# Routed expert tiles: the up product with the weights stationary and 128 tokens moving

## What is computed

```python
shared = silu(xf @ shared_w1.T) * (xf @ shared_w2.T) @ shared_w3.T
scores = sigmoid(xf @ router_w.T)
_, top_idx = top_k(scores + expert_bias, 2)          # 8 experts
...
# each token passes through its two experts, weighted by its gate:
# gate * ((silu(x @ w1_e.T) * (x @ w2_e.T)) @ w3_e.T),  256 hidden units per expert
```

## Time and profile before

| | |
|---|---|
| median of 3 executions | 1747.06 us (1745.62 to 1749.57) |
| the profiled execution | 1750.36 us, span 1748.3 us |
| mean granted TensorE clock | 0.984 |
| busy, share of the span: PE, DVE, ACT, POOL | 94%, 65%, 49%, 39% |
| tile steps, first pass | about 257 to 436 us |
| tile steps, second pass | about 1030 to 1217 us |

### The profile page before, as it was taken

The page is one execution under the profiler, slowest core; times in us unless marked ns, Lnnn a source line. Parts: engine busy times, 40 slices in busy tenths (PEclk is TensorE's granted clock), DMA queues, the critical chain, the costliest instruction groups (busy, mean ns, idle before and its releaser), DMA issues.

```text
span 1748.3 us, 42002 instructions
## 1 busy us (share of the span) xinstructions
PE 1650.5 (94%) x14972; PEld 1109.8 (63%) x14973; DVE 1142.2 (65%) x2498; ACT 857.5 (49%) x1475; POOL 682.4 (39%) x655
## 2 busy tenths in 40 slices
PE   6999999999989999989899999999799979998999
PEld 3565656666567767665555656666466657776666
DVE  6677766666466666657765556665577477777675
ACT  4355434443466566644344334443366455664764
POOL 2342323443122222132333324433244587887243
PEclk9999999999989999999999999999899999998999
DMA  7132323332211111003210123332332033131011
GB/s 251 49 108 83 106 74 103 109 111 91 52 38 36 24 24 24 1 1 94 85 38 34 39 67 111 110 112 83 80 67 42 1 75 74 40 76 39 14 36 48
DMA packets 90149, 115.82 MB, mean 66 GB/s; under 512 B 9296, under 2 KB 76400, under 8 KB 90032
## 3 DMA queue, kind: packets, MB, share of 16 engines
q1 hardware_dynamic: 68624, 70.25, 14.5%
q0 software_dynamic: 21408, 43.93, 9.0%
HBM read 66.24 MB, written 47.90 MB: 65 GB/s over the span
## 4 chain that ended last, share of the span: by engine, by line
PE 57%; DVE 6%; POOL 4%; ACT 3%; issue 2%; DMA 0%; DVEq 0%; SPq 0%; ACTq 0%; POOLq 0%
PE ps L1675 10%; PE ps L1677 10%; PE ps L1676 10%; PE ps L1909 3%; PE ps L1908 3%; PE ps L1691 2%; PE ps L2006 2%; PE ps L1890 2%; PE ps L1891 2%; PE ps L2163 2%; PE ps L2145 1%; PE ps L2011 1%; PE ps L2133 1%; POOL work L746 1%; PE ps L1970 1%
## 5 line engine op out<-in xcount | busy, mean ns | idle before, releaser
L703 POOL DMA_INDIRECT routed<-work x142 | 136.1, 959 | 234.9 <-DVE work L1431 229.8
L1675 PE MATMUL ps<-later_hi,work 128*128 (+1 forms) x632 | 203.2, 322 | 1.2 <-ACT work L1044 1.0
L1676 PE MATMUL ps<-later_lo,work 128*128 (+1 forms) x632 | 203.1, 321 | 0.0
L1677 PE MATMUL ps<-later_hi,work 128*128 (+1 forms) x632 | 203.0, 321 | 0.0
L1675 PE MATMUL ps<-xt_hi,wsh 128*128 128x512 f16 x512 | 194.9, 381 | 4.7 <-DVEq L1185 2.2
L1676 PE MATMUL ps<-xt_lo,wsh 128*128 128x512 f16 x512 | 194.9, 381 | 0.0
L1677 PE MATMUL ps<-xt_hi,wsh 128*128 128x512 f16 x512 | 194.8, 380 | 0.0
L640 POOL TENSOR_TENSOR rstd<-mv,eps 128x4 f32<-128x4 f32 x49 | 15.2, 309 | 409.1 <-DVE mv L1140 398.4
L854 ACT ACTIVATE work<-ps 128x512 f32<-128x512 f32 x128 | 76.4, 597 | 181.5 <-PE ps L1677 170.8
L1675 PE MATMUL ps<-wsh,work 128*128 128x256 f16 x512 | 140.7, 275 | 4.8 <-ACT work L843 2.7
L1324 DVE SCALAR_TENSOR_TENSOR work<-ps,work 128x512 f32<-128x512 f32 x128 | 88.1, 689 | 84.4 <-ACT work L854 69.1
(11 more groups left out here) (246 smaller groups left out, 4257.0 us busy)
## 6 DMA issues: line engine op xcount, KB each, us to landing
work<-expert_x SPq DMA_DIRECT2D x142, 129.0 KB
yg<-in_w_later SPq DMA_DIRECT2D x9, 496.0 KB
w1q<-in_w_later SPq DMA_DIRECT2D x9, 496.0 KB
yg<-routed SPq DMA_DIRECT2D x8, 512.0 KB, 3.7
yg<-routed POOLq DMA_DIRECT2D x8, 512.0 KB, 6.0
yg<-in_w SPq DMA_DIRECT2D x8, 512.0 KB
later_hi<-routed SPq DMA_DIRECT2D x8, 512.0 KB, 3.8
later_hi<-routed POOLq DMA_DIRECT2D x8, 512.0 KB, 5.9
```

Of the source, the lines that this page charges most:

```text
L703: nc.gpsimd.indirect_dma_start(routed[:, :], bass.IndirectOffsetOnAxis(m.homes[:, i:i + 1], 0), m.t_y[:, i % 4, :], None).then_inc(s[f"til ...
L1675: nc.tensor.matmul(out_, a[0], b[0], start=start, stop=False)
L1676: nc.tensor.matmul(out_, a[0], b[1], start=False, stop=False)
L1677: return nc.tensor.matmul(out_, a[1], b[0], start=False, stop=stop)
```

## The change

The up product is made the other way round. For each of the 4 slices f of 128 units and each k, the expert's weights (128 features x 128 units) are stationary and the tile's 128 tokens move: 4 x 2 x 3 = 24 matmuls of 128 columns. The result has units on partitions, which is what the down product needs as its stationary operand, so the two second transposes, their semaphore `th_turned` and the use of PSUM banks 4 and 5 go. ACT and DVE split the product in SBUF. The gate belongs to a token, and the tokens now lie along the row in the product, so it is no longer a per-partition factor there: one small DVE operation per tile scales it into `m.gates`, and it multiplies the output at L1431, where tokens are on partitions again. The constant HS / WS takes its place in the product. DVE waits before the product for `th_lo` of two tiles earlier; ACT waits for `tile_prod` instead of `th_turned`. The arithmetic is otherwise the same.

```diff
--- before.py
+++ after.py
@@ -230,7 +230,7 @@
...
-                        "tile_hi tile_lo tile_up tile_silu tile_prod th_turned th_hi th_lo tile_down tile_y tile_out0 "
+                        "tile_hi tile_lo tile_up tile_silu tile_prod th_hi th_lo tile_down tile_y tile_out0 "
...
@@ -321,6 +321,7 @@
             m.more = r([NE, NSEQ * TPS])
             m.tile_x, m.zeros = r([4, RW]), r([RW])
             m.homes = r([TILES], I32)
+            m.gates = r([4])
             m.xn = (xn, m.tile_x)
             m.over, m.sums = r([TILES, NE]), r([2, TILES])
             m.before = r([NE, NE])
@@ -896,10 +897,10 @@
                         nc.scalar.activation(m.t_silu[:, v], ps[:, 2 + v, 0:HE], ACT.Silu, scale=1 / WS).then_inc(s["tile_silu"], 1)
                     if has(2):
                         j, v = i - 2, u % 2
-                        act.wait_ge(s["th_turned"], j + 1 + T0)
+                        act.wait_ge(s["tile_prod"], j + 1 + T0)
                         if not isinstance(j, int) or j >= 2:
                             act.wait_ge(s["tile_down"], j - 1 + T0)
-                        nc.scalar.activation(m.th_hi[:, v], ps[:, 4 + v, 0:EU * P].rearrange("p (k t) -> p k t", k=EU),
+                        nc.scalar.activation(m.th_hi[:, v].rearrange("p k t -> p (k t)"), m.t_prod[:, v],
                                              ACT.Copy).then_inc(s["th_hi"], 1)
                 each_tile(act, step, 2)
                 body(NSEQ - 1, 1)
@@ -1414,21 +1415,23 @@
                         j, v = i - 1, (u - 1) % 2
                         dve.wait_ge(s["tile_silu"], j + 1 + T0)
                         if not isinstance(j, int) or j >= 2:
-                            dve.wait_ge(s["th_turned"], j - 1 + T0)
-                        nc.vector.scalar_tensor_tensor(out=m.t_prod[:, v], in0=ps[:, 2 + v, HE:2 * HE],
-                                                       scalar=m.tile_x[:, (u - 1) % 4, D:D + 1], in1=m.t_silu[:, v],
+                            dve.wait_ge(s["th_lo"], j - 1 + T0)
+                        nc.vector.tensor_scalar(m.gates[:, (u - 1) % 4:(u - 1) % 4 + 1], m.tile_x[:, (u - 1) % 4, D:D + 1],
+                                                0.5 / (HS * HS), None, ALU.mult)
+                        nc.vector.scalar_tensor_tensor(out=m.t_prod[:, v], in0=ps[:, 2 + v, HE:2 * HE], scalar=HS / WS,
+                                                       in1=m.t_silu[:, v],
                                                        op0=ALU.mult, op1=ALU.mult).then_inc(s["tile_prod"], 1)
                     if has(2):
                         j, v = i - 2, u % 2
                         dve.wait_ge(s["th_hi"], j + 1 + T0)
-                        nc.vector.tensor_tensor(m.th_lo[:, v], ps[:, 4 + v, 0:EU * P].rearrange("p (k t) -> p k t", k=EU),
-                                                m.th_hi[:, v], ALU.subtract).then_inc(s["th_lo"], 1)
+                        nc.vector.tensor_tensor(m.th_lo[:, v].rearrange("p k t -> p (k t)"), m.t_prod[:, v],
+                                                m.th_hi[:, v].rearrange("p k t -> p (k t)"), ALU.subtract).then_inc(s["th_lo"], 1)
                     if has(3):
                         j, v = i - 3, (u - 3) % 4
                         dve.wait_ge(s["tile_down"], j + 1 + T0)
                         if not isinstance(j, int) or j >= 4:
                             dve.wait_ge(s[f"tile_out{v}"], 16 * (b - (1 if u < 3 else 0)) + in_slot(v) * earlier(n))
-                        nc.vector.tensor_scalar(m.t_y[:, v], ps[:, 6 + v % 2, 0:D], 0.5 / (WS * HS), None,
+                        nc.vector.tensor_scalar(m.t_y[:, v], ps[:, 6 + v % 2, 0:D], m.gates[:, v:v + 1], None,
                                                 ALU.mult).then_inc(s["tile_y"], 1)
                 sequences_before_tiles(dve, body)
                 assert done[0] == TAB_STEPS
@@ -1835,18 +1838,13 @@
                         pe.wait_ge(s["tile_lo"], j + 1 + T0)
                         if not isinstance(j, int) or j >= 2:
                             pe.wait_ge(s["tile_prod"], j - 1 + T0)
-                        for k in range(KT):
-                            ins = mm3(ps[:, 2 + v, :], (m.t_hi[:, v, k], m.t_lo[:, v, k]),
-                                      both(wup, ds(at + k * NE * 2 * HE, 2 * HE)), k == 0, k == KT - 1)
+                        for f in range(2 * EU):
+                            for k in range(KT):
+                                ins = mm3(ps[:, 2 + v, f * P:(f + 1) * P], both(wup, ds(at + k * NE * 2 * HE + f * P, P)),
+                                          (m.t_hi[:, v, k], m.t_lo[:, v, k]), k == 0, k == KT - 1)
                         ins.then_inc(s["tile_up"], 1)
                     if has(0):
                         pe.load(own_columns[u], m.table[0:1, ds(TILES + i, 1)])
-                    if has(2):
-                        j, v = i - 2, u % 2
-                        pe.wait_ge(s["tile_prod"], j + 1 + T0)
-                        for k in range(EU):
-                            ins = nc.tensor.transpose(ps[:, 4 + v, k * P:(k + 1) * P], m.t_prod[:, v, k * P:(k + 1) * P], ident)
-                        ins.then_inc(s["th_turned"], 1)
                     if has(3):
                         j, v = i - 3, (u - 3) % 2
                         at = columns(u, 3)
```

## The result

The changed kernel takes 1906.97 us in the median of 4 runs (1904.66 to 1910.24), beside 1747.84 for the kernel before in 4 runs on the same chip: ratio 1.0913, interval 1.0891 to 1.0934. The forecast was 1907.0. The profiled execution took 1904.66, its span is 1902.7; before it was 1750.36 and 1748.3, so the two profiled executions differ by 154.3 us, where the medians differ by 159.1.

The account below looks back on a forecast made before the run. PE's array was taken to pace each tile at 2.39 us, and after the change PE's sequencer at 3.61. Loops 146 us plus unrolled steps 18 less 4 gave +160, so 1907 us, range 1800 to 1965.

Parts of the forecast that it names:

- The bound changes from array to sequencer: Routed tiles: PE's sequencer at 3.61 us per tile exceeds the array's 2.22 and becomes the bound; chance 0.76.
- A group costs 0.235: PE's sequencer: each weight-address group takes 0.235 us; six more groups per tile add 1.41 us.
- lower bound: PE's sequencer: an address group takes at least its two instructions' own 46 + 32 = 78 ns.
- The cycle, 3.61: PE's sequencer per tile in the loops: 2.23 + 1.41 - 0.03 = 3.61 us, against 2.39 before.
- The table load: PE's sequencer between up and down groups: the load takes 0.44 us, within a stretch of 0.97.
- 146 + 18 - 4 = 160: Both tile passes: 146 us in loops, 18 in unrolled steps, less 4 for the sequencer's lead at pass starts.
- The signs: Marks of a right forecast: period near 3.6 us, ten FUSED_REGOPS per tile, "issue" idle before groups, clock 1.00.
- VectorE at nothing: DVE's added gate operation, 0.165 us per tile, costs nothing while the sequencer leads; otherwise nothing to 0.05 us per tile.
- Instruction fetch: Whole program: 83 blocks of 16 KB grow by some 5, costing nothing, at most 2 us.
- A: Rival, tile passes: the array stays the bound, groups under 0.096 us; -24 us, 1723; chance 0.09.
- B: Rival, up product: short matmuls do not hide weight loads, 81 ns per pair; +62 us, 1809; chance 0.06.
- C: Rival, tile passes: the sequencer starves PE and the clock falls to 1.2 GHz; +290 us, 2035; chance 0.07.

Follow-up runs that it names:

- run 1: Changed kernel with constant up weight addresses, every tile using expert 0's up weights: 1758.07 us, ratio 1.0018 to the kernel before.
- run 2: Kernel before with each 512-column up matmul cut into four of 128, each with its own address: 1921.25 us, ratio 1.0954.
- run 6: Low part of tile k-2 earlier: on run 1 1727.2 us, on the kernel before 1745.01, on the change with packed additions 1730.18 (1736.71 without the early order).
- Runs 3 and 4: Changed kernel with addresses packed in stretches (up 1802.4 us, up and down 1785.55), and with each address one unpacked addition (1896.43 us).
- run 7: Kernel before with only the gate moved to the output and the gates' small operation added: 1743.97 us, ratio 0.9995.
- packed_early: Whole change with addresses as packed single additions, and the low part of tile k-2 ahead of tile k-1's product: 1730.18 us, ratio 0.9919.
- fixed_early: Changed kernel with constant up addresses (expert 0) and the low part of tile k-2 ahead of tile k-1's product: 1727.2 us, ratio 0.990.
- run 5: Changed kernel with packed addresses and one six-entry table load per four tiles: 1825.04 us; with the low part earlier too, 1801.89 us.
- hoist_all: Changed kernel with the up and the down address calculations each packed in one stretch: 1785.55 us, ratio 1.019.
- packed: Whole change with addresses as packed single additions, low part in the change's own order: 1736.71 us, ratio 0.9953.
- adds: Changed kernel with the table in bytes, each address one addition and none packed: 1896.43 us, ratio 1.0864.
- hoist_load: Changed kernel with packed addresses and one table load of six entries per four tiles: 1825.04 us, ratio 1.0457.

## Why the prediction was right, point by point

**The bound changes from array to sequencer: shown.** Taking the up addresses away gives back 149 of 159 us (run 1), adding them to the kernel before costs 169 (run 2, against the 1751.82 of the kernel before on that chip), and four packed instructions for twenty turn the loss into a gain (run 6).

**A group costs 0.235: as forecast.** The groups stand 0.235 apart and there are ten per tile. I had not said what in it costs. Runs 3 and 4 show that it is the number of instructions, not of calculations, so the lower bound by the instructions' own 46 + 32 ns was no real case: a group of two lone additions of 32 ns still takes 0.226.

**The cycle, 3.61: it was 3.57** in the loop of the first pass (mean over 56 tiles) and 3.60 in the second, and 3.31 where I took 3.3 in the unrolled steps. Two terms were off, in opposite directions. The table load was too large: I took 0.44 for it from one tile; over all tiles it is 0.306, and in the array-bound kernel before it lasted 297 to 551 ns (median 308). The groups were too small: by the starts of the sequencer's instructions the ten take 2.44 us per tile in the mean, not 2.35. The sum of the passes was forecast as 146 + 18 - 4 = 160 and is 156.

**1907.0 against 1906.97: the last digits are luck.** The mechanism and the period were forecast, to about 1%. The profiled executions differ by 154.3 us and the medians by 159.1, the runs of the changed kernel alone spread over 5.6 us, and the two errors in the cycle partly cancel.

**The signs.** The period, the ten FUSED_REGOPS per tile, the groups 0.235 apart, the gap of 0.6 us between up and down and the clock of 1.00 came as written. One sign was badly chosen: idle time with "issue" before each group does not stand in the view, since the modelled ends cover it.

**VectorE at nothing: right, with a wrong reason in it.** I wrote "a few ns either way" for the output's scaling. By shape, VectorE of the changed kernel and then of the kernel before (count, busy us, mean ns, idle before):

```profile
L1434 DVE TENSOR_SCALAR work<-ps,work 128x256 f32<-128x256 f32 x142 | 68.7, 484 | 40.8 <-PE ps L1680 39.7
L1421 DVE SCALAR_TENSOR_TENSOR work<-ps,work 128x256 f32<-128x256 f32 x142 | 58.8, 414 | 0.0
L1419 DVE TENSOR_SCALAR work<-work 128x1 f32<-128x1 f32 x142 | 21.8, 154 | 174.0 <-ACT work L897 174.0
```

```profile
L1418 DVE SCALAR_TENSOR_TENSOR work<-ps,work 128x256 f32<-128x256 f32 x142 | 68.7, 484 | 98.3 <-ACT work L896 88.6 <-PE ps L1848 9.7
L1431 DVE TENSOR_SCALAR work<-ps 128x256 f32<-128x256 f32 x142 | 58.8, 414 | 5.6 <-PE ps L1677 5.5
```

The operation that takes its scalar from memory costs 484 ns and the one with a constant 414, whichever they are. The change moves that scalar from the product to the output, so 70 ns go on one side and come on the other, and only the gates' 154 ns remain. They cost nothing in the kernel before (run 7).

**Instruction fetch: right.** 83 blocks became 88, the five that I had estimated.

**The rivals.** A (array stays bound) would have shown a period near 2.2 without gaps; there are gaps, and packed_early shows what it would have taken. B (loads not hidden) is refuted by 56 ns between matmuls at 403.02 to 403.19, and not only in such a short lead: fixed_early keeps tiles of 2.21 us with PE busy in 40.00 of 40 us. The 81 ns per pair that B adds up from 25.4 and 56 would make a tile of 2.83 us. C (the clock falls) did not come in the changed kernel: the granted clock of the stretch is 1.00 with PE busy 33 of 40 us and pauses of 0.8 us at most. It did come in run 5, where PE stood for 1.8 of 2.2 us and the clock then was 0.50, so this rival was not far off. No view gives the 2.4 and 1.2 GHz that I wrote beside the clock: what the traces show is 512 columns per 0.216 us at a clock of 1.00, 2.37 per ns, and 128 columns per 0.107 us at 0.50 (run 5), 1.20 per ns.

**What stays open.** In run 1, what holds the 54th silu and PE's sequencer in both passes is not known. In hoist_all, on the same chip, the 54th silu of both passes is 1.4 us late too; in fixed_early and packed, on other chips, it is on time. After the first late silu, every second silu starts 0.8 to 1.1 us after the modelled end of its up product, with ScalarE idle and no earlier instruction in its way. That it recurs in step with the late low part is seen; what makes it recur is not. And what lies outside the passes, where these kernels are alike, took 1412.6 us of the span in the kernel before, 1421.8 in run 1 and 1407.8 in fixed_early. So 9 us of run 1's miss are not from the tiles. Two things go with them: the kernel before is itself slower on run 1's chip (1751.82 us against 1743.53 on fixed_early's), and the mean granted clock is 0.982 in run 1 and 0.988 in fixed_early, that is, by estimate, some 63 and 41 us at half clock. Whether that is all of it was not tested.

## What to carry to other kernels

Where a TensorE operand's address depends on a register, count the address instructions per microsecond of matmul as you count columns: cutting a matmul in four to exchange its operands multiplies them, and at 128 columns a group of three lasts 0.17 us while its two instructions take 0.235. Then make each address one addition (keep the table in bytes, with its alignment declared) and calculate them in one stretch, which in run 6 put 16 additions into three instructions. It takes both here: additions alone gave 0.09 us per tile and packing alone 0.98, the two together 1.24. When a bound has been lifted, look at the next one before counting the gain: here it was an input that came only 0.7 us before its turn.

## What the runs showed of the hardware that I had not expected

- PE's sequencer pays per instruction. Lone additions stand 0.113 us apart with matmuls between them (adds); the three instructions that hold 16 additions last 60 to 85 ns, 79 in the median, and start 0.138 apart (packed_early).
- A register load on PE's sequencer takes 0.306 us for one entry and 1.712 for six, which is 0.285 per entry.
- VectorE's product and its scaling of the output, both on 128x256, take 484 ns with the scalar from memory and 414 with a constant.
- After PE had stood for 1.8 of 2.2 us in hoist_load the granted clock was 0.50 for the next 3.4 us, though not after each such pause; in the changed kernel, with pauses of 0.6 to 0.8 us in every tile, it stayed at 1.00 in all tile loops.
- After a silu that came 1.6 us late, and in another place after one that came 0.8 us late, a pipeline with 0.76 us of slack ran in a slower rhythm (2.21 and mostly 2.7 to 2.8 in turn). Twice it lasted to the end of the pass, some 15 tiles on; once it ended by itself after some 30 tiles.
